# The tile stage of a gated attention and mixture-of-experts kernel: another order within a tile, no index copies, loops written out

## The chip, the cores and the metric

The kernel runs on one core of a Trainium2 chip. The metric is the device time of one execution in microseconds; for the kernel before it is the median of three runs, 376.43 us (375.81 to 379.23).

## What is computed

A block of a gated Flamingo layer over x, 8 x 256 x 256 floats: a retention attention on a normalised x, added to x through a tanh gate, then a mixture of 8 experts of which each token uses 2, added through a second gate. The change touches the second half only:

```python
scores = softmax(xf @ Wg.T); expert_weights, expert_indices = top_k(scores, 2)
gates = (one_hot(expert_indices, 8) * expert_weights[..., None]).sum(axis=1)
h1 = lora_in(xf, W1, b1, A1, B1)     # 256 -> 512, per expert
h3 = lora_in(xf, W3, b3, A3, B3)
g = silu(h1) * h3
y_e = lora_out(g, W2, b2, A2, B2)    # 512 -> 256
y = einsum('te,ted->td', gates, y_e)
x = x + tanh(g_ffn) * y
```

xf is the normalised x, 2048 tokens.

## The kernel before

The kernel has three stages. In the first, some 130 us, the attention runs batch by batch, and the experts' weights are loaded, their low-rank parts added, and each weight split into a high part (WH) and a low part (WL) that stay on the chip. Then a short routing step sorts the tokens by expert into 39 tiles of 128 token slots (NT_SLOTS), each tile for one expert; it leaves for tile i one column of row indices to gather (`gidx`), one of row indices to scatter to (`sidx`), and the expert's number (`eid`). The last slots may be padding.

The third is the tile stage, from 152 us on. For each tile:
- GpSimd gathers 128 normalised rows into `xg` (four buffers, XBUF; L735), three tiles ahead, and scatters a finished tile `ys` with an addition into the output rows (L747). A scatter waits for the landing of the one before it, since two tiles can add to one row. Ahead of each, the index column is copied to a small tile of its own (`gi` L732, `si` L743), and GpSimd waits for its copy.
- TensorE transposes x (`x_transposes`, L473), multiplies by the weights of h1 and of h3 (`up`, L483, each in three passes: xh and xl by WH, xb by WL), transposes g (`g_transposes`, L491) and multiplies by W2 (`down`, L500, gh, gl, gb).
- ScalarE makes xh and xb from the x transposes (L645, L646), gh from the g transposes and gb from gh (L651, L653), the silu (L662), and the bias of the result into `ys` (L669). The last waits for the scatter that still reads that one of the two ys buffers.
- VectorE makes xl (L997) and gl (L1001), adds the biases to h1 and h3 (L1006), multiplies them (L1012), works out the token's gate (L989, L991), and finishes `ys` (L1018).

Every engine runs its own list in the order written; semaphores join them. `tile_steps` writes 4 tiles, then a loop of 8 turns with 4 tiles each, then 3 tiles; in the loop the tile number is a register, and so are the values waited for. The order within tile i, as each engine has it (each works on parts of three tiles):
- TensorE: x transposes of i+1, up h1 of i, g transposes of i-1, up h3 of i, down of i-1.
- ScalarE: xh and xb of i+1, gh and gb of i-1, silu of i, bias of ys of i.
- VectorE: xl of i+1, gate of i+1, bias of h1 of i, gl of i-1, bias of h3 and product of i, ys of i-1.
- GpSimd: gather of i+3, scatter of i-1.

Of the kernel before, what the change touches and what calls it, by code (L numbers as in the profile page):

```python
# [29 lines left out]
U32 = mybir.dt.uint32  # L30
# [37 lines left out]
def flamingo(nc, x, ctxT, wqkv, tables, mask, gates_in, w_all, lora, biases, wgT, ident_in, consts, out):  # L68
# [9 lines left out]
    with whole:  # L78
# [78 lines left out]
        tiles = ExitStack()  # L157
        gi = [sb(tiles, f"gi{p}", [P, 1], U32) for p in range(2)]
        si = [sb(tiles, f"si{p}", [P, 1], U32) for p in range(2)]
        xg = [sb(tiles, f"xg{q}", [P, D + K]) for q in range(XBUF)]  # L160
# [39 lines left out]
        s_gates, s_gates_d, s_g0, s_gs = sem("s_gates"), sem("s_gates_d"), sem("s_g0"), sem("s_gs")  # L200
        s_gi, s_si = sem("s_gi"), sem("s_si")
        s_xg = [sem(f"s_xg{q}") for q in range(XBUF)]
# [22 lines left out]
        def tile_steps(engine, step):  # L225

            turns = (NT_SLOTS - XBUF - (XBUF - 1)) // XBUF
            for i in range(XBUF):
                step(i, i, i == 0, True)
            with engine.Fori(1, turns + 1) as r:  # L230
                for q in range(XBUF):
                    step(XBUF * r + q, q, False, True)
            for i in range(XBUF * (turns + 1), NT_SLOTS):
                step(i, i % XBUF, False, i + 1 < NT_SLOTS)

# [100 lines left out]
        def _(pe):  # L336
# [129 lines left out]
            def x_transposes(i, q):  # L466
                pe.wait_ge(s_xg[q], 16 * ((i - q) // XBUF + 1))
                if not isinstance(i, int) or i > 0:
# [42 lines left out]
            def read_expert(i, q):  # L511
                pe.reg_load(regs[q], eid[0:1, bass.ds(i, 1)])

            def tile(i, q, first, more):
                p = q % 2
                if more and not first:
                    x_transposes(i + 1, (q + 1) % XBUF)
                e = expert(q)
                up(pH1, i, p, e, 0, s_h1)
                if first:  # L520
                    x_transposes(1, 1)
                if not first:
                    g_transposes(i - 1)
                up(pH3, i, p, e, 1, s_h3)
# [14 lines left out]
        def _(act):  # L539
# [107 lines left out]

            def g_parts(i):
                act.wait_ge(s_gT, i + 1)
                pos_wait(act, s_y, i)  # L650
                nc.scalar.activation(gh[:], pG[:, :], ACT.Copy).then_inc(s_gh, 1)  # L651
                act.wait_ge(s_gh, i + 1)
                nc.scalar.activation(gb[:], gh[:].bitcast(F32), ACT.Copy).then_inc(s_gb, 1)  # L653

            def tile(i, q, first, more):
                p = q % 2
                if more:
                    x_parts(i + 1, 1 - p)
                if not first:
                    g_parts(i - 1)  # L660
                act.wait_ge(s_h1b, i + 1)
                nc.scalar.activation(h1[:], h1[:], ACT.Silu).then_inc(s_silu, 1)  # L662

                e = act.value_load(eid[0:1, bass.ds(i, 1)], min_val=0, max_val=E - 1)
                act.wait_ge(s_gs, i + 1)
                if not isinstance(i, int) or i >= 2:
                    settle(act)
                    act.wait_ge(s_scat[p], 16 * half(i, p))
# [6 lines left out]
            tile_steps(act, tile)  # L675
            g_parts(NT_SLOTS - 1)


        @block.gpsimd
        def _(pool):  # L680
# [44 lines left out]

            def gather(i, q):
                pos_wait(pool, s_xT, i - XBUF + 1)
                pos_wait(pool, s_gs, i - XBUF + 1)
                p = q % 2
                if not isinstance(i, int) or i >= 2:  # L730
                    pool.wait_ge(s_xg[(q + 2) % XBUF], 16 * ((i - 2 - (q + 2) % XBUF) // XBUF + 1))
                nc.gpsimd.tensor_copy(gi[p][:], gidx[:, bass.ds(i, 1)]).then_inc(s_gi, 1)  # L732
                pool.wait_ge(s_gi, i + 1)
                settle(pool)
                nc.gpsimd.indirect_dma_start(out=xg[q][:], out_offset=None, in_=xn2_d,  # L735
                                             in_offset=bass.IndirectOffsetOnAxis(ap=gi[p][:, 0:1], axis=0)
                                             ).then_inc(s_xg[q], 16)

            def scatter(i, p):

                if not isinstance(i, int) or i >= 1:
                    pool.wait_ge(s_scat[1 - p], 16 * ((i + p) // 2))
# [4 lines left out]
                nc.gpsimd.indirect_dma_start(out=out_rows, out_offset=bass.IndirectOffsetOnAxis(ap=si[p][:, 0:1], axis=0),  # L747
                                             in_=ys[p][:], in_offset=None, bounds_check=TOK - 1,
                                             oob_is_err=False, compute_op=ALU.add).then_inc(s_scat[p], 16)
# [3 lines left out]
            for i in range(XBUF - 1):  # L753
                gather(i, i)

            def tile(i, q, first, more):

                if not isinstance(i, int) or i + XBUF - 1 < NT_SLOTS:
                    gather(i + (XBUF - 1), (q + XBUF - 1) % XBUF)
                if not first:  # L760
                    scatter(i - 1, (q + 1) % 2)

            tile_steps(pool, tile)
            scatter(NT_SLOTS - 1, (NT_SLOTS - 1) % 2)


        @block.vector
        def _(dve):
# [216 lines left out]
            def gates_of(i, q):  # L985

                dve.wait_ge(s_xg[q], 16 * ((i - q) // XBUF + 1))
                pos_wait(dve, s_gs, i)
                nc.vector.tensor_tensor(g0, xg[q][:, D:D + 1], is0[:, bass.ds(i, 1)], ALU.mult).then_inc(s_g0, 1)  # L989
                dve.wait_ge(s_g0, i + 1)  # L990
                nc.vector.scalar_tensor_tensor(gs[q], xg[q][:, D + 1:D + 2], is1[:, bass.ds(i, 1)], g0,  # L991
                                               ALU.mult, ALU.add).then_inc(s_gs, 1)
# [119 lines left out]
```

## Time and profile before

| | us |
|---|---|
| median of three runs | 376.43 |
| the profiled execution | 375.73 |
| its span, first to last instruction | 373.9 |
| TensorE matmuls busy | 310.2 (83%) |
| VectorE busy | 262.3 (70%) |
| GpSimd busy | 209.6 (56%) |
| ScalarE busy | 186.1 (50%) |
| DMA in the chain that ended last | 34% |

The profile is of one execution. Engines are named PE (matmuls), PEld (TensorE's weight loads), DVE (VectorE), ACT (ScalarE), POOL (GpSimd). The granted TensorE clock is at its full level in the whole tile stage from 163 us on. A scatter or gather shows up twice: as an instruction on POOL, which is the time in which GpSimd writes out what is to be moved, and in the chain of waits as "DMA", from the start of that instruction to the landing of the data.

### The profile page before, as it was taken

To read this page: it belongs to the slowest core of one execution; us is meant where nothing else is said; L and a number is where in the kernel's file an instruction comes from. 1 tells how busy PE (TensorE), PEld (TensorE's weight loads), DVE (VectorE), ACT (ScalarE), POOL (GpSimd) and SP (SyncE) were. 2 spreads that over 40 slices of the span, in tenths; PEclk is the share of its full clock that TensorE was granted. 3 is DMA by queue.
4 is the path that set the end of the run, shared out by engine and by line. 5 is a ranking of instruction groups with operands and counts; after the bars stand their busy time and mean duration, and the time that the engine had idled before them with its cause. 6 is when DMAs were issued, how large, how long until landed. Compare 5 with 4: busy or idle time off the path is not lost.

```text
span 373.9 us, 7655 instructions
## 1 busy us (share of the span) xinstructions
PE 310.2 (83%) x1680; PEld 232.8 (62%) x1701; DVE 262.3 (70%) x639; ACT 186.1 (50%) x372; POOL 209.6 (56%) x247
## 2 busy tenths in 40 slices
PE   2869779989987723299999999999999999999970
PEld 1747667767766512157765777777777767677750
DVE  1667878898896689357675677776778767777750
ACT  4634645554655422065455555565555555455630
POOL 0456577777687436425465556656556556556441
PEclk9989999999998855579999999999999999999997
DMA  7779999678566449511332323322331323333200
GB/s 257 223 226 319 314 292 283 197 216 254 184 202 199 134 107 297 211 45 28 59 44 39 56 44 47 51 47 52 53 56 29 56 45 53 56 43 50 28 2 1
DMA packets 27887, 45.78 MB, mean 122 GB/s; under 512 B 6528, under 2 KB 15104, under 8 KB 27360
## 3 DMA queue, kind: packets, MB, share of 16 engines
q1 hardware_dynamic: 15408, 28.52, 24.2%
q0 software_dynamic: 7488, 9.36, 15.5%
q10 hardware_dynamic: 4976, 7.74, 6.9%
q8 instruction: 6, 0.10, 0.1%
q14 instruction: 9, 0.07, 0.1%
HBM read 33.65 MB, written 12.86 MB: 124 GB/s over the span
## 4 chain that ended last, share of the span: by engine, by line
DMA 34%; PE 20%; issue 13%; DVE 13%; ACT 7%; POOL 7%; POOLq 2%; DVEq 1%; SPq 1%; ACTq 0%
DMA out<-ys,si 26%; PE bank L483 3%; PE bank L393 3%; DMA LS<-lora_parts 3%; POOL WL L683 3%; PE bank L427 2%; PE bank L500 2%; DVE gl L1001 2%; DMA WH<-lora_in 2%; DVE h L1006 2%; PE bank L349 2%; DMA stage<-w_all_in 2%; DVE g L1006 1%; ACT xn L575 1%; PE bank L420 1%
## 5 line engine op out<-in xcount | busy, mean ns | idle before, releaser
L747 POOL DMA_INDIRECT out<-ys,si x39 | 62.5, 1603 | 45.8 <-POOL si L743 26.2
L683 POOL TENSOR_TENSOR WL<-stage,WH 128x512 f32 (+1 forms) x48 | 60.3, 1271 | 31.4 <-ACT WH L570 31.4
L735 POOL DMA_INDIRECT xg<-xn_rows,gi x39 | 39.5, 1013 | 32.6 <-POOL gi L732 32.6
L483 PE MATMUL bank<-WH,xh 128*128 x156 | 56.7, 445 | 0.7 <-ACT xh L645 0.7
L997 DVE TENSOR_TENSOR xl<-bank,xh 128x256 fp32r<-128x256 f32 x39 | 16.6, 425 | 48.6 <-ACT xb L646 48.6
L483 PE MATMUL bank<-WH,xl 128*128 x156 | 49.5, 399 | 0.0
L669 ACT ACTIVATE ys<-BB,gsel 128x256 f32 x39 | 19.8, 509 | 57.4 <-DMA out<-ys,si 57.1
L483 PE MATMUL bank<-WL,xb 128*128 x136 | 43.2, 388 | 1.6 <-issue 0.2
L570 ACT ACTIVATE WH<-stage 128x512 f32 (+1 forms) x48 | 29.0, 625 | 28.7 <-DVE stage L773 28.7
L651 ACT ACTIVATE gh<-bank 128x512 fp32r<-128x512 f32 x39 | 23.3, 598 | 26.5 <-PE bank L491 26.5
L483 PEld LDWEIGHTS bank<-WH,xl 128*128 128x128 f32 x156 | 29.8, 191 | 6.7 <-DVE xl L997 0.2
L773 DVE TENSOR_TENSOR stage<-bank,stage 128x512 f32<-128x512 f32 x48 | 31.3, 680 | 3.8 <-DMA stage<-w_all_in 2.9
L500 PE MATMUL bank<-WH,gh 128*128 x156 | 32.1, 328 | 0.9 <-ACT gh L651 0.9
L500 PE MATMUL bank<-WH,gl 128*128 x156 | 27.1, 296 | 3.7 <-DVE gl L1001 2.6
L1012 DVE TENSOR_TENSOR g<-g,h 128x512 f32<-128x512 f32 x39 | 27.0, 693 | 4.1
L732 POOL COPY gi<-gidx 128x1 uint32 (+1 forms) x39 | 27.2, 699 | 2.8 <-DVE sidx L980 2.7
L1006 DVE TENSOR_TENSOR h<-bank,BB 128x512 f32<-128x512 f32 x39 | 27.0, 691 | 2.5 <-PE bank L483 1.0
L500 PEld LDWEIGHTS bank<-WH,gh 128*128 128x128 f32 x156 | 24.0, 189 | 7.0 <-issue 1.8
L1006 DVE TENSOR_TENSOR g<-bank,BB 128x512 f32<-128x512 f32 x39 | 26.7, 686 | 1.9 <-PE bank L483 1.1
L1001 DVE TENSOR_TENSOR gl<-bank,gh 128x512 fp32r<-128x512 f32 x39 | 26.7, 683 | 2.0 <-ACT gh L651 1.5
L483 PEld LDWEIGHTS bank<-WH,xh 128*128 128x128 f32 x156 | 24.4, 193 | 2.7 <-issue 2.3
L500 PEld LDWEIGHTS bank<-WH,gl 128*128 128x128 f32 x156 | 20.9, 188 | 8.0 <-DVE gl L1001 7.7
(132 smaller groups left out, 619.3 us busy)
## 6 DMA issues: line engine op xcount, KB each, us to landing
stage<-w_all_in SPq DMA_DIRECT2D x48, 256.0 KB, 4.0
BB<-biases_in SPq DMA_DIRECT2D x8, 640.0 KB, 9.7
LS<-lora_parts SPq DMA_DIRECT2D x24, 144.0 KB, 3.0
lora_parts<-WH ACTq DMA_DIRECT2D x3, 864.0 KB, 9.4
xs<-x_in SPq DMA_DIRECT2D x8, 256.0 KB, 3.8
cx<-ctxT_in SPq DMA_DIRECT2D x8, 256.0 KB, 4.1
out<-x ACTq DMA_DIRECT2D x8, 256.0 KB, 2.3
xn_rows<-xn ACTq DMA_DIRECT2D x8, 256.0 KB, 4.2
```

Of the source, the lines that this page charges most:

```text
L483: last = nc.tensor.matmul(dst[:, :], lhs[p][:, c * P:(c + 1) * P], W[:, bass.ds(e * (UNITS * UC) + (2 * kind + c) * UC, HID)], start=(part ...
L500: last = nc.tensor.matmul(pY[:, 0:D], lhs[:, c * P:(c + 1) * P], W[:, bass.ds(e * (UNITS * UC) + 4 * UC + c * D, D)], start=(part == 0 and ...
L570: nc.scalar.activation(w_dst(WH, s, m), stage[(u * UNITS + m) % NSTAGE][:], ACT.Copy).then_inc(s_wh, 1)
L651: nc.scalar.activation(gh[:], pG[:, :], ACT.Copy).then_inc(s_gh, 1)
L683: nc.gpsimd.tensor_tensor(w_dst(WL, s, m), stage[(u * UNITS + m) % NSTAGE][:], w_dst(WH, s, m).bitcast(F32), ALU.subtract).then_inc(s_wl, 1)
L732: nc.gpsimd.tensor_copy(gi[p][:], gidx[:, bass.ds(i, 1)]).then_inc(s_gi, 1)
L735: nc.gpsimd.indirect_dma_start(out=xg[q][:], out_offset=None, in_=xn2_d, in_offset=bass.IndirectOffsetOnAxis(ap=gi[p][:, 0:1], axis=0)).th ...
L747: nc.gpsimd.indirect_dma_start(out=out_rows, out_offset=bass.IndirectOffsetOnAxis(ap=si[p][:, 0:1], axis=0), in_=ys[p][:], in_offset=None, ...
L773: nc.vector.tensor_tensor(stage[b][:], pW[m % 2][:, :], stage[b][:], ALU.add).then_inc(s_add, 1)
L1001: nc.vector.tensor_tensor(gl[:], pG[:, :], gh[:].bitcast(F32), ALU.subtract).then_inc(s_gl, 1)
L1006: nc.vector.tensor_tensor(dst[:], src[:, :], b, ALU.add).then_inc(sig, 1)
L1012: nc.vector.tensor_tensor(g[:], g[:], h1[:], ALU.mult).then_inc(s_g, 1)
```

## The change

1. `tile_steps` writes out all 39 tiles; tile numbers and the values waited for become constants. GpSimd's own loop likewise.
2. The index copies `gi` and `si` and their semaphores go; gather and scatter take a column of `gidx` and `sidx` directly. One of the gather's waits goes too.
3. The order within a tile:
   - TensorE: up h1 of i, g transposes of i-1, x transposes of i+1, up h3 of i, down of i-1.
   - ScalarE: gh of i-1, xh and xb of i+1, gb of i-1, then as before.
   - VectorE: gate of i+1, bias of h1, gl of i-1, xl of i+1, bias of h3 and product, ys of i-1.

```diff
         def tile_steps(engine, step):
 
-            turns = (NT_SLOTS - XBUF - (XBUF - 1)) // XBUF
-            for i in range(XBUF):
-                step(i, i, i == 0, True)
-            with engine.Fori(1, turns + 1) as r:
-                for q in range(XBUF):
-                    step(XBUF * r + q, q, False, True)
-            for i in range(XBUF * (turns + 1), NT_SLOTS):
-                step(i, i % XBUF, False, i + 1 < NT_SLOTS)
+            for i in range(NT_SLOTS):
+                step(i, i % XBUF, i == 0, i + 1 < NT_SLOTS)
...
             def tile(i, q, first, more):
                 p = q % 2
-                if more and not first:
-                    x_transposes(i + 1, (q + 1) % XBUF)
-                e = expert(q)
-                up(pH1, i, p, e, 0, s_h1)
-                if first:
-                    x_transposes(1, 1)
+                up(pH1, i, p, expert(q), 0, s_h1)
                 if not first:
                     g_transposes(i - 1)
-                up(pH3, i, p, e, 1, s_h3)
+                if more:
+                    x_transposes(i + 1, (q + 1) % XBUF)
+                up(pH3, i, p, expert(q), 1, s_h3)
...
-            def g_parts(i):
+            def g_high(i):
                 act.wait_ge(s_gT, i + 1)
                 pos_wait(act, s_y, i)
                 nc.scalar.activation(gh[:], pG[:, :], ACT.Copy).then_inc(s_gh, 1)
+
+            def g_short(i):
                 act.wait_ge(s_gh, i + 1)
                 nc.scalar.activation(gb[:], gh[:].bitcast(F32), ACT.Copy).then_inc(s_gb, 1)
 
             def tile(i, q, first, more):
                 p = q % 2
+                if not first:
+                    g_high(i - 1)
                 if more:
                     x_parts(i + 1, 1 - p)
                 if not first:
-                    g_parts(i - 1)
+                    g_short(i - 1)
...
-            def gather(i, q):
-                pos_wait(pool, s_xT, i - XBUF + 1)
-                pos_wait(pool, s_gs, i - XBUF + 1)
-                p = q % 2
-                if not isinstance(i, int) or i >= 2:
-                    pool.wait_ge(s_xg[(q + 2) % XBUF], 16 * ((i - 2 - (q + 2) % XBUF) // XBUF + 1))
-                nc.gpsimd.tensor_copy(gi[p][:], gidx[:, bass.ds(i, 1)]).then_inc(s_gi, 1)
-                pool.wait_ge(s_gi, i + 1)
-                settle(pool)
+            def gather(i):
+
+                q = i % XBUF
+                if i >= XBUF:
+                    pool.wait_ge(s_xT, i - XBUF + 1)
+                    pool.wait_ge(s_gs, i - XBUF + 1)
                 nc.gpsimd.indirect_dma_start(out=xg[q][:], out_offset=None, in_=xn2_d,
-                                             in_offset=bass.IndirectOffsetOnAxis(ap=gi[p][:, 0:1], axis=0)
+                                             in_offset=bass.IndirectOffsetOnAxis(ap=gidx[:, i:i + 1], axis=0)
                                              ).then_inc(s_xg[q], 16)
 
-            def scatter(i, p):
-
-                if not isinstance(i, int) or i >= 1:
+            def scatter(i):
+
+                p = i % 2
+                if i >= 1:
                     pool.wait_ge(s_scat[1 - p], 16 * ((i + p) // 2))
-                nc.gpsimd.tensor_copy(si[p][:], sidx[:, bass.ds(i, 1)]).then_inc(s_si, 1)
-                pool.wait_ge(s_si, i + 1)
                 pool.wait_ge(s_ys, i + 1)
-                settle(pool)
...
             def tile(i, q, first, more):
                 p = q % 2
-                e = dve.value_load(eid[0:1, bass.ds(i, 1)], min_val=0, max_val=E - 1)
+                e = dve.value_load(eid[0:1, i:i + 1], min_val=0, max_val=E - 1)
                 if more:
-                    x_rest(i + 1, 1 - p)
                     gates_of(i + 1, (q + 1) % XBUF)
                 pos_wait(dve, s_g, i)
                 biased(h1, pH1, i, e, 0, s_h1, s_h1b)
                 if not first:
                     g_rest(i - 1)
+                if more:
+                    x_rest(i + 1, 1 - p)
                 product(i, e)
```

## Rows read from the trace of the kernel before

**Rows 1.** The page: busy time by engine, and the chain by line.
```profile
PE 310.2 (83%) x1680; PEld 232.8 (62%) x1701; DVE 262.3 (70%) x639; ACT 186.1 (50%) x372; POOL 209.6 (56%) x247
...
DMA out<-ys,si 26%; PE bank L483 3%; PE bank L393 3%; DMA LS<-lora_parts 3%; POOL WL L683 3%; PE bank L427 2%; PE bank L500 2%; DVE gl L1001 2%; DMA WH<-lora_in 2%; DVE h L1006 2%; PE bank L349 2%; DMA stage<-w_all_in 2%; DVE g L1006 1%; ACT xn L575 1%; PE bank L420 1%
```

**Rows 2.** Chain of waits around 220 us: start us, us, what.
```profile
217.67 0.46 DVE ys L1018
...
219.01 3.78 DMA out<-ys,si
...
222.94 0.19 POOL si L743
...
224.06 3.81 DMA out<-ys,si
```

**Rows 3.** Timeline of TensorE, 270 to 280 us: start us, us, instructions merged.
```profile
270.12 0.60 PE L491 MATMUL bank<-ident,g 128*128 128x128 f32 x4
...
272.40 0.64 PE L500 MATMUL bank<-WH,gl 128*128 x4
272.88 0.61 PE L500 MATMUL bank<-WL,gb 128*128 x4
...
273.47 0.72 PE L483 MATMUL bank<-WH,xh 128*128 x2
...
274.94 0.60 PE L491 MATMUL bank<-ident,g 128*128 128x128 f32 x4
```

**Rows 4.** Timeline of TensorE, 279 to 285 us.
```profile
280.19 0.60 PE L491 MATMUL bank<-ident,g 128*128 128x128 f32 x4
...
283.35 0.61 PE L500 MATMUL bank<-WL,gb 128*128 x4
...
284.35 0.73 PE L483 MATMUL bank<-WH,xh 128*128 x2
```

**Rows 5.** Timeline of TensorE, first and last but one g transposes.
```profile
165.47 0.66 PE L491 MATMUL bank<-ident,g 128*128 128x128 f32 x4
...
356.51 0.60 PE L491 MATMUL bank<-ident,g 128*128 128x128 f32 x4
```

**Rows 6.** Waits of weight loads, 165 to 357 us: total us, times, longest.
```profile
PEld bank L500 <- DVE gl L1001: 7.7, 20, 1.0
```

**Rows 7.** Timeline of ScalarE and VectorE, 270 to 277 us; in brackets idle time before.
```profile
271.56 0.68 DVE L1001 TENSOR_TENSOR gl<-bank,gh 128x512 fp32r<-128x512 f32 x1
...
274.15 0.51 ACT L669 ACTIVATE ys<-BB,gsel 128x256 f32 x1 [1.61 <-DMA out<-ys,si]
...
275.57 0.60 ACT L651 ACTIVATE gh<-bank 128x512 fp32r<-128x512 f32 x1 [0.37 <-PE bank L491]
...
276.76 0.68 DVE L1001 TENSOR_TENSOR gl<-bank,gh 128x512 fp32r<-128x512 f32 x1
```

**Rows 8.** Timeline of GpSimd: a scatter, the gather behind it, the last scatter.
```profile
275.29 1.61 POOL L747 DMA_INDIRECT out<-ys,si  x1 [0.93 <-POOL si L743]
...
277.93 1.01 POOL L735 DMA_INDIRECT xg<-xn_rows,gi  x1 [0.84 <-POOL gi L732]
...
365.61 1.57 POOL L747 DMA_INDIRECT out<-ys,si  x1 [1.23 <-issue]
```

**Rows 9.** Timeline of GpSimd: the first gather.
```profile
153.60 1.17 POOL L735 DMA_INDIRECT xg<-xn_rows,gi  x1 [1.00 <-POOL gi L732]
```

**Rows 10.** Chain of waits, 180 to 204 us: the two late landings.
```profile
180.70 4.72 DMA out<-ys,si
...
196.90 5.67 DMA out<-ys,si
```

**Rows 11.** DMA queues, 152 to 374 us: the queue of code: packets, MB, share.
```profile
q8 instruction: 4, 0.07, 0.1%
```

**Rows 12.** DMA queues, 183 to 184 us.
```profile
q8 instruction: 1, 0.02, 7.6%
```

**Rows 13.** Chain of waits, 360 to 374 us: the last scatter but one.
```profile
361.38 2.76 DMA out<-ys,si
```

More of the change, by code:

```diff
@@ L157, in flamingo @@
         tiles = ExitStack()
-        gi = [sb(tiles, f"gi{p}", [P, 1], U32) for p in range(2)]
-        si = [sb(tiles, f"si{p}", [P, 1], U32) for p in range(2)]
         xg = [sb(tiles, f"xg{q}", [P, D + K]) for q in range(XBUF)]
@@ L200, in flamingo @@
         s_gates, s_gates_d, s_g0, s_gs = sem("s_gates"), sem("s_gates_d"), sem("s_g0"), sem("s_gs")
-        s_gi, s_si = sem("s_gi"), sem("s_si")
         s_xg = [sem(f"s_xg{q}") for q in range(XBUF)]
@@ L467, in x_transposes @@
                 pe.wait_ge(s_xg[q], 16 * ((i - q) // XBUF + 1))
-                if not isinstance(i, int) or i > 0:
+                if i > 0:
                     pe.wait_ge(s_xh, i)
@@ L511, in read_expert @@
             def read_expert(i, q):
-                pe.reg_load(regs[q], eid[0:1, bass.ds(i, 1)])
+                pe.reg_load(regs[q], eid[0:1, i:i + 1])
             def tile(i, q, first, more):
                 p = q % 2
-                if more and not first:
-                    x_transposes(i + 1, (q + 1) % XBUF)
-                e = expert(q)
-                up(pH1, i, p, e, 0, s_h1)
-                if first:
-                    x_transposes(1, 1)
+                up(pH1, i, p, expert(q), 0, s_h1)
                 if not first:
                     g_transposes(i - 1)
-                up(pH3, i, p, e, 1, s_h3)
+                if more:
+                    x_transposes(i + 1, (q + 1) % XBUF)
+                up(pH3, i, p, expert(q), 1, s_h3)
                 if more:
@@ L659, in tile @@
                 if not first:
-                    g_parts(i - 1)
+                    g_short(i - 1)
                 act.wait_ge(s_h1b, i + 1)
                 nc.scalar.activation(h1[:], h1[:], ACT.Silu).then_inc(s_silu, 1)
-                e = act.value_load(eid[0:1, bass.ds(i, 1)], min_val=0, max_val=E - 1)
+                e = act.value_load(eid[0:1, i:i + 1], min_val=0, max_val=E - 1)
                 act.wait_ge(s_gs, i + 1)
-                if not isinstance(i, int) or i >= 2:
-                    settle(act)
+                if i >= 2:
                     act.wait_ge(s_scat[p], 16 * half(i, p))
@@ L675, in _ @@
             tile_steps(act, tile)
-            g_parts(NT_SLOTS - 1)
+            g_high(NT_SLOTS - 1)
+            g_short(NT_SLOTS - 1)
         @block.gpsimd
@@ L723, in _ @@
                                         ALU.mult).then_inc(s_atj, 1)
-            def gather(i, q):
-                pos_wait(pool, s_xT, i - XBUF + 1)
-                pos_wait(pool, s_gs, i - XBUF + 1)
-                p = q % 2
-                if not isinstance(i, int) or i >= 2:
-                    pool.wait_ge(s_xg[(q + 2) % XBUF], 16 * ((i - 2 - (q + 2) % XBUF) // XBUF + 1))
-                nc.gpsimd.tensor_copy(gi[p][:], gidx[:, bass.ds(i, 1)]).then_inc(s_gi, 1)
-                pool.wait_ge(s_gi, i + 1)
-                settle(pool)
+            def gather(i):
[3 more added lines that the diff above has]
+                    pool.wait_ge(s_gs, i - XBUF + 1)
                 nc.gpsimd.indirect_dma_start(out=xg[q][:], out_offset=None, in_=xn2_d,
-                                             in_offset=bass.IndirectOffsetOnAxis(ap=gi[p][:, 0:1], axis=0)
+                                             in_offset=bass.IndirectOffsetOnAxis(ap=gidx[:, i:i + 1], axis=0)
                                              ).then_inc(s_xg[q], 16)
-            def scatter(i, p):
-                if not isinstance(i, int) or i >= 1:
+            def scatter(i):
+                p = i % 2
+                if i >= 1:
                     pool.wait_ge(s_scat[1 - p], 16 * ((i + p) // 2))
-                nc.gpsimd.tensor_copy(si[p][:], sidx[:, bass.ds(i, 1)]).then_inc(s_si, 1)
-                pool.wait_ge(s_si, i + 1)
                 pool.wait_ge(s_ys, i + 1)
-                settle(pool)
-                nc.gpsimd.indirect_dma_start(out=out_rows, out_offset=bass.IndirectOffsetOnAxis(ap=si[p][:, 0:1], axis=0),
+                nc.gpsimd.indirect_dma_start(out=out_rows, out_offset=bass.IndirectOffsetOnAxis(ap=sidx[:, i:i + 1], axis=0),
                                              in_=ys[p][:], in_offset=None, bounds_check=TOK - 1,
@@ L753, in _ @@
             for i in range(XBUF - 1):
[L754 to L764, printed above, removed]
+                gather(i)
+            for i in range(NT_SLOTS):
+                if i + XBUF - 1 < NT_SLOTS:
+                    gather(i + XBUF - 1)
+                if i >= 1:
+                    scatter(i - 1)
+            scatter(NT_SLOTS - 1)
         @block.vector
@@ L988, in gates_of @@
                 pos_wait(dve, s_gs, i)
-                nc.vector.tensor_tensor(g0, xg[q][:, D:D + 1], is0[:, bass.ds(i, 1)], ALU.mult).then_inc(s_g0, 1)
+                nc.vector.tensor_tensor(g0, xg[q][:, D:D + 1], is0[:, i:i + 1], ALU.mult).then_inc(s_g0, 1)
                 dve.wait_ge(s_g0, i + 1)
-                nc.vector.scalar_tensor_tensor(gs[q], xg[q][:, D + 1:D + 2], is1[:, bass.ds(i, 1)], g0,
+                nc.vector.scalar_tensor_tensor(gs[q], xg[q][:, D + 1:D + 2], is1[:, i:i + 1], g0,
                                                ALU.mult, ALU.add).then_inc(s_gs, 1)
```

## Prediction, made before the changed kernel was run

> **What bounds the kernel now.** I read the page first: TensorE is busy for 83% of the span, yet the largest item of the chain that ended last is the landing of the scatter, 26% [rows 1]. Both can't be the bound alone, so I went to the tile stage, the stretch that the change touches, and read the chain of waits there, then each engine's timeline.
>
> The chain shows a loop that closes on itself [rows 2]. A scatter starts at 219.01 and lands 3.78 us later, at 222.79; GpSimd then copies the index (0.19), and the next scatter starts at 224.06, 5.05 us after the first. So landing to start is 1.27 us with the index copy. Where the scatter is released by VectorE's ys instead, ys ends at 218.13 and the scatter starts at 219.01: 0.88 us with no copy between. The loop is serial by its own wait (scatter i waits for scatter i-1).
>
> TensorE has a loop of its own. The reader should compare the starts of the g transposes, one set per tile [rows 3, 4]: 270.12 to 274.94 is 4.82 us, 274.94 to 280.19 is 5.25. The long tile is one in which gl came late; in the stage 20 of TensorE's weight loads waited for gl, 7.7 us in all [rows 6]. At the back edge of the written loop there is another loss: the last matmuls of down start at 283.35 and the next up at 284.35, 1.00 us, where the same step takes 0.59 inside a turn (272.88 to 273.47): 0.41 us in each of 8 turns. The mean distance over the stage, from 165.47 to 356.51 for 37 distances, is 191.04 / 37 = 5.16 us [rows 5]; the best are 4.8.
>
> Why gl is late [rows 7]: ScalarE is in order, and its ys for the tile (274.15) waits for a scatter's landing; behind it stand xh and xb, behind these VectorE's xl, the two gate operations, the bias of h, and only then gl (276.76 to 277.44). Relative to the g transposes gl ends 2.50 us later here, and 2.12 in the unstalled tile (272.24 - 270.12), where TensorE starts on it after 2.28. So the serial scatters (5.05 us) bound the stage, and TensorE (4.8) follows close behind.
>
> **The change part by part.** The sum is made against the profiled execution, 375.73 us (span 373.9 and 1.8 around it); the median of the runs shown, 376.43, is 0.7 above it.
>
> Index copy out of the scatter. Landing to start falls from 1.27 to about 0.88 us, as where ys released it and no copy lay between [rows 2]; the register move and the dispatch stay. The loop becomes 3.80 + 0.88 = 4.68 us against 5.05. Bounds: at least the copy itself goes (0.19, loop 4.86); at most half of what is left of the 0.88 goes too (loop 4.3). I take 4.68, the nearest row.
>
> Index copy out of the gather. The gather takes 1.01 us and starts 2.64 us after the scatter (275.29, 277.93) [rows 8]. It lies under the scatter's 3.8 us landing and costs nothing in either version; without that cover it would cost about 1.8 us a tile. Without the copy it can start at the end of the scatter's own 1.61, which is what rival C is about. At the entry the first gather loses its copy (0.19, as the scatter's) and the 1.00 idle behind it [rows 9] shrinks towards the 0.88 above: -0.3 us, on the path to the first tile.
>
> Loops written out. The 0.41 at each back edge goes (8 x 0.41 = 3.3 us, part of the difference between 5.16 and 4.8, not added to it). Register arithmetic for i, branches and the extra semaphore increments go too. TensorE reads the expert's register twice per tile, one short move more, covered by matmuls (bounds 0 and 0.05 x 39 = 2 us; I take 0, since such moves stand between matmuls now without a gap). What is added is code to fetch; see below.
>
> The new order. Count from the g transposes of a tile. TensorE: g transposes 0, x transposes 0.35, up of h3 about 0.55, gh 1.85, gl 2.5, gb 3.0, next up 3.45, g transposes again 4.8: the same instructions as before, so the same 4.8. ScalarE: gh starts at 0.63 as now (275.57 - 274.94) and ends at 1.23; xh and xb follow to 1.8, gb (as long as gh) to 2.4, needed at 3.0; silu to 3.1. VectorE: the gates; the bias of h from 0.2 to 0.9, since it no longer stands behind xl; gl (0.68) from 1.26 to 1.95, needed at 2.5; then xl, needed only at 4.1 by the next up; bias of h3 when its matmuls end (2.05 to 2.7); product to 3.5, needed at 4.8; result when the last gb matmul has ended, to 4.1. VectorE is busy for 4 us of a tile, below 4.8. What stands behind the moved waits: behind ScalarE's wait for the g transposes the x parts, with 2 us to spare; behind VectorE's wait for xb the bias of h3 and the product, with 0.4 and 1.3.
>
> How late may a scatter be? With ys ended at 4.1 it starts at 5.0 and lands at 8.8; ScalarE's ys behind it ends at 9.5, its next gh is due at 9.6 + 0.63 = 10.2: 0.75 us to spare there and 0.55 at gl, 1.3 in all before TensorE stalls.
>
> Code to fetch. The stage has 11 tile bodies of code for its 39 tiles (4, a loop of 4, 3), and four fetches of 16 KB fall in it [rows 11]; with 39 bodies it is about 14. What one can do [rows 10, 12]: a fetch lies at 183 us in a scatter's data, and that scatter landed after 4.72 us instead of 3.8; the one of 196.90 landed after 5.67, with a fetch in its wait too. The other two fetches cost no landing. So I estimate that half of 14 hit, 7 x 0.9 = 6.3 us late in all. Cover: 1.3 us once and 34 x (4.79 - 4.68) = 3.7 us that the shorter scatter loop makes up. Left: 1.3; with one hit of the dearer kind (0.9 more) 2.2, so a tile costs 4.79 + 0.06 = 4.85.
>
> A page of the Trainium skill, "Runtime: NRT & Kernel Launch", section "Instruction fetch mechanics", says that code is streamed ahead in 16 KiB blocks and that crossing a block is mostly hidden, while a taken branch outside the window stalls. By that rule the stage would take 37 x 4.79 = 177.2 us and the kernel 361.7. The trace agrees for TensorE, which shows no gap at 183 us, and not for the scatter (4.72).
>
> The end. The last scatter but one starts at 361.38 and lands 2.76 later, at 364.14; the last starts at 365.61, 1.47 after that [rows 8, 13]. With 0.88 it starts 0.6 earlier. The 8.3 us behind it (to 373.9) are untouched.
>
> Sum: entry -0.3; stage 37 x 4.85 = 179.4 against 191.0, -11.6; end -0.6: **-12.5 us**. 375.73 - 12.5 = 363.2, and with the 0.7 between that execution and the median 363.9 us.
>
> **The rivals.**
> A, every large fetch hits a scatter: 14 x 0.9 = 12.6 us late, 5.0 covered, 7.6 left on 177.2. The stage takes 184.8, -6.2, and the kernel 376.4 - 6.2 - 0.9 = 369.3. For it: blocks may follow each other at the same phase of every third tile. Against it: two of four hit now.
> B, no change: each fetch costs a scatter 1.4 on average, between the two that are seen (0.9, 1.9): 19.6 - 5.0 = 14.6, the stage 191.8, and the kernel 376.3. The same comes out if any wait of the new order makes each tile 0.3 us late.
> The skill's page "DMA: Bandwidth & Descriptors", section "Queues, rings and completion order", says that an engine takes turns between its queues packet by packet; by it a scatter's small packet can stand behind 16 KB, and A and B stay open. The 4.72 agrees.
> C, slower: the gather starts right behind the scatter, 1.6 us after it instead of 2.64, and its rows mix with the scatter's. Price: up to 1.0 us a landing, the time by which it moves. At 0.75 the scatter loop is 3.8 + 0.75 + 0.88 = 5.43 against 5.16, 34 x 0.27 = +9.2, -0.9 at the ends: 384.7. It decides from 0.5 a landing, where the loop is 5.18. Against it: one engine issues both to one queue, the scatter first.
>
> **How the numbers follow.** My forecast 0.60 (own range 361 to 367), A 0.18, B 0.12, C 0.10. The predicted time is 363.9. The low end is that of no fetch cost, 361.7, and 0.06 us a tile less on TensorE (2.2 us), since up of h1 no longer begins on the x transposes: 359.5. The high end takes in A and a quarter of the way on to B: 371. About 1% (3.8 us) is what a measurement of this kernel can tell from no change: faster is my case and A, 0.78; the same is B, 0.12; slower is C, 0.10.
>
> **What would show it.** Right: distances between g transposes of 4.8 to 4.9, no weight load waiting for gl, landing to next scatter 0.9, landings still 3.8 but scatters often released by ys; some 14 fetches of 16 KB, the long tiles beside them. Wrong: landings above 4.3 in every tile (C); scatter distances of 5.1 with a late landing every third tile (A, B); TensorE gaps before loads that nothing in the trace released.

## The result, and the profile after

| | before | after |
|---|---|---|
| median, us | 376.12 (4 runs) | 363.69 (4 runs, 361.68 to 365.32) |
| ratio | | 0.965, 95% interval 0.958 to 0.972 |
| the profiled execution | 375.73 | 365.32 |
| its span | 373.9 | 363.5 |

The changed kernel is 12.4 us faster. The profiled execution of it happens to be the longest of the four, which matters below. The ratios below leave out slow executions (over 1.5% above the fastest of their kernel) and the medians do not, and the profiles of no_copies_old_order (372.49 us) and pe_loop (367.11) are of slow ones.

The page, busy time by engine and the chain by line:

```profile
PE 305.6 (84%) x1680; PEld 232.8 (64%) x1700; DVE 266.3 (73%) x638; ACT 179.2 (49%) x371; POOL 192.6 (53%) x169
...
PE bank L474 29%; PE bank L491 15%; PE bank L482 5%; PE bank L418 4%; PE bank L384 3%; PE bank L464 2%; POOL WL L675 2%; DMA WH<-lora_in 2%; PE bank L340 2%; PE bank L411 2%; PE bank L393 1%; PE bank L429 1%; DMA LS<-lora_parts 1%; DVE WH L798 1%; ACT xn L563 1%
```

Where the scatter's landing held 26% of the chain [rows 1], it is gone from the list, and up (L474), down (L491) and the g transposes (L482) stand in its place. The chain of waits around 275 us (start us, us, what) is TensorE alone, where [rows 2] had one scatter after another:

```profile
273.20 1.38 PE bank L474 x6
274.58 0.44 PE bank L482 x4
275.02 0.22 PE bank L464 x2
275.24 1.39 PE bank L474 x6
276.63 1.41 PE bank L491 x12
278.04 1.38 PE bank L474 x6
279.42 0.44 PE bank L482 x4
```

These pieces close without a gap: 274.58 to 279.42 is one tile, 4.84 us. VectorE and ScalarE of the same tile show the new order (timeline; in brackets the idle time before and what ended it):

```profile
274.17 0.51 ACT L660 ACTIVATE ys<-BB,gsel 128x256 f32 x1 [1.75 <-DMA out<-ys,sidx]
...
274.42 0.60 PE L482 MATMUL bank<-ident,g 128*128 128x128 f32 x4
...
274.81 0.69 DVE L989 TENSOR_TENSOR h<-bank,BB 128x512 f32<-128x512 f32 x1 [0.42 <-PE bank L474]
...
275.06 0.60 ACT L639 ACTIVATE gh<-bank 128x512 fp32r<-128x512 f32 x1 [0.38 <-PE bank L482]
...
275.69 0.69 DVE L984 TENSOR_TENSOR gl<-bank,gh 128x512 fp32r<-128x512 f32 x1 [0.19 <-ACT gh L639]
...
276.31 0.43 DVE L980 TENSOR_TENSOR xl<-bank,xh 128x256 fp32r<-128x256 f32 x1
...
276.95 0.64 PE L491 MATMUL bank<-WH,gl 128*128 x4
```

gl ends 1.96 us after the g transposes began (276.38 - 274.42) and TensorE starts on it after 2.53; before it ended after 2.50 in a stalled tile [rows 7]. ScalarE's ys still waits for a scatter (1.75 us), but the wait now ends 0.9 us ahead of gh. GpSimd's timeline:

```profile
195.72 1.59 POOL L734 DMA_INDIRECT out<-ys,sidx  x1 [1.95 <-DVE gsel L974]
197.61 0.99 POOL L724 DMA_INDIRECT xg<-xn_rows,gidx  x1 [0.31 <-issue]
201.88 1.59 POOL L734 DMA_INDIRECT out<-ys,sidx  x1 [3.28 <-DMA out<-ys,sidx]
203.78 0.99 POOL L724 DMA_INDIRECT xg<-xn_rows,gidx  x1 [0.30 <-issue]
206.51 1.59 POOL L734 DMA_INDIRECT out<-ys,sidx  x1 [1.75 <-DMA out<-ys,sidx]
```

The gather follows its scatter after 1.89 us instead of 2.64 [rows 8]. The scatter of 195.72 is a late one: its landing took 5.3 us, so the next one, at 201.88, is late too. The one after that, at 206.51, already makes up for it: 4.63 us behind the one before, where TensorE's tile takes 4.83.

Where the 10.4 us between the two spans went, by the same marks (first gather; first and last but one g transposes; last scatter):

| stretch | before | after | difference |
|---|---|---|---|
| start to first gather | 153.6 | 155.3 | +1.7 |
| to the first g transposes | 11.9 | 11.1 | -0.8 |
| 37 distances of g transposes | 191.0 | 180.5 | -10.6 |
| to the last scatter | 9.1 | 8.4 | -0.7 |
| to the end | 8.3 | 8.2 | 0 |

The first row mixes two things. The gather's copy is gone, which took 1.0 us off (see the entry below); the code before it is the same in both kernels and took 2.7 us more in this execution, which is not the change's. Over all profiled executions of this study the first gather started after 151.6 to 158.7 us. The -0.8 of the second row is not firm either: the same kernel once more took 12.0 us there (after_again, below). So I compare kernels by the 37 distances, and by medians only where several us are at stake.

### The profile page after: what moved, and what is told of

Its sections match the earlier page's. It is cut to its first block, busy times and chain, and to the rows that moved or that the text cites. A ratio compares the mean times of both kernels' runs of the same rounds, so it can differ in the third digit from the quotient of the medians.

```text
span 363.5 us, 7072 instructions
## 1 busy us (share of the span) xinstructions
PE 305.6 (84%) x1680; PEld 232.8 (64%) x1700; DVE 266.3 (73%) x638; ACT 179.2 (49%) x371; POOL 192.6 (53%) x169
## 4 chain that ended last, share of the span: by engine, by line
PE 69%; DVE 7%; POOL 5%; DMA 5%; issue 5%; ACT 4%; SPq 1%; ACTq 1%; POOLq 1%; DVEq 0%
PE bank L474 29%; PE bank L491 15%; PE bank L482 5%; PE bank L418 4%; PE bank L384 3%; PE bank L464 2%; POOL WL L675 2%; DMA WH<-lora_in 2%; PE bank L340 2%; PE bank L411 2%; PE bank L393 1%; PE bank L429 1%; DMA LS<-lora_parts 1%; DVE WH L798 1%; ACT xn L563 1%
## 5 line engine op out<-in xcount | busy, mean ns | idle before, releaser
L734 POOL DMA_INDIRECT out<-ys,sidx x39 | 61.8, 1585 | 88.4 <-DVE gsel L974 58.0
L474 PE MATMUL bank<-WH,xh 128*128 x156 | 56.5, 443 | 0.7 <-ACT xh L633 0.7
L474 PE MATMUL bank<-WH,xl 128*128 x156 | 49.2, 397 | 0.0
L724 POOL DMA_INDIRECT xg<-xn_rows,gidx x39 | 38.7, 992 | 15.5 <-issue 11.3
L474 PE MATMUL bank<-WL,xb 128*128 x136 | 43.0, 386 | 1.6 <-issue 0.2
L984 DVE TENSOR_TENSOR gl<-bank,gh 128x512 fp32r<-128x512 f32 x39 | 27.0, 691 | 10.6 <-ACT gh L639 10.6
L474 PEld LDWEIGHTS bank<-WH,xl 128*128 128x128 f32 x156 | 29.5, 189 | 7.4 <-DVE xl L980 0.2
L491 PE MATMUL bank<-WH,gh 128*128 x156 | 32.2, 328 | 1.0 <-ACT gh L639 0.9
L491 PEld LDWEIGHTS bank<-WH,gh 128*128 128x128 f32 x156 | 24.0, 189 | 7.8 <-issue 2.7
L474 PEld LDWEIGHTS bank<-WH,xh 128*128 128x128 f32 x156 | 23.9, 192 | 2.3 <-issue 1.8
L643 ACT ACTIVATE gb<-gh 128x512 bf16<-128x512 f32 x39 | 25.0, 641 | 0.1
L654 ACT ACTIVATE h<-h 128x512 f32<-128x512 f32 x39 | 25.0, 641 | 0.0
L482 PEld LDWEIGHTS bank<-ident,g 128*128 128x128 f32 x156 | 19.3, 140 | 8.8 <-DVE g L995 1.7
L491 PE MATMUL bank<-WH,gl 128*128 x156 | 24.9, 281 | 0.0
```

Source lines behind the costliest of these rows:

```text
L474: last = nc.tensor.matmul(dst[:, :], lhs[p][:, c * P:(c + 1) * P], W[:, bass.ds(e * (UNITS * UC) + (2 * kind + c) * UC, HID)], start=(part ...
L482: last = nc.tensor.transpose(pG[:, c * P:(c + 1) * P], g[:, c * P:(c + 1) * P], ident[:])
L491: last = nc.tensor.matmul(pY[:, 0:D], lhs[:, c * P:(c + 1) * P], W[:, bass.ds(e * (UNITS * UC) + 4 * UC + c * D, D)], start=(part == 0 and ...
L984: nc.vector.tensor_tensor(gl[:], pG[:, :], gh[:].bitcast(F32), ALU.subtract).then_inc(s_gl, 1)
```

## The experiments

Two questions: which part of the change carried the gain, and whether the account of two loops (scatters in series, TensorE close behind) is what happens. Each number of "37 distances" is from the first to the last but one g transposes in TensorE's timeline, as in [rows 5], in one profiled execution of each kernel. A late landing is one of more than 4.3 us.

### One part at a time

**order_only**: the kernel before with the new order in its loops; TensorE, ScalarE and VectorE as in the change, the rest untouched.

```diff
                 p = q % 2
-                if more and not first:
-                    x_transposes(i + 1, (q + 1) % XBUF)
-                e = expert(q)
-                up(pH1, i, p, e, 0, s_h1)
+                up(pH1, i, p, expert(q), 0, s_h1)
                 if not first:
                     g_transposes(i - 1)
+                if more:
+                    x_transposes(i + 1, (q + 1) % XBUF)
...
```

> Only the new order within a tile; loops and index copies stay as before. Theory (two loops, the longer sets the tile: scatters in series at 5.06 us with the copy, TensorE at 4.8): the scatter loop is untouched, so a tile still takes 5.06 to 5.1 instead of 5.16, gl is no longer late, and the gain is 2 to 4 us: 372 to 374 us. Rival (the order alone is what brought the gain, by freeing gl): 363 to 366 us, tiles of 4.85.

**written_out**: the kernel before with tile_steps written out; copies and order stay.

```diff
-            with engine.Fori(1, turns + 1) as r:
-                for q in range(XBUF):
-                    step(XBUF * r + q, q, False, True)
...
+            for i in range(NT_SLOTS):
+                step(i, i % XBUF, i == 0, i + 1 < NT_SLOTS)
```

> Only the loops written out; copies and old order stay. Theory: the back edge's 0.41 us on TensorE goes, but the scatters still follow each other every 5.06 us, and late landings beside code fetches are no longer made up: no gain, 374 to 378 us. Rival (loop control was the cost): 8 x 0.41 = 3.3 us and more off, 370 to 372 us with tiles below 5.0.

**written_order**: both of these; only the index copies, and with them the semaphore increment behind each copy (`settle`) and one of the gather's waits, differ from the changed kernel.

> Loops written out and the new order, but the index copies kept: the whole change but one part. Theory: the scatter loop with its copy (1.27 us from landing to start) sets the tile, 5.06 us, 371 to 375 us. Rival (the copies were hidden): as the changed kernel, 362 to 365 us, tiles of 4.83.

**no_copies_old_order**: the changed kernel with the old order on the three engines.

```diff
                 if more:
+                    x_rest(i + 1, 1 - p)
                     gates_of(i + 1, (q + 1) % XBUF)
                 pos_wait(dve, s_g, i)
                 biased(h1, pH1, i, e, 0, s_h1, s_h1b)
                 if not first:
                     g_rest(i - 1)
-                if more:
-                    x_rest(i + 1, 1 - p)
...
```

> Loops written out and copies gone, but the old order within a tile. Theory: scatters can follow each other every 4.65 us, TensorE sets the tile at 4.8 to 4.9 if gl comes in time, since ScalarE's ys is released earlier: 363 to 367 us, some loads still waiting for gl. Rival (the order is needed for TensorE to run without stalls): tiles above 5.0, 369 us or more.

| kernel | written out | copies gone | new order | 37 distances | a tile, mean | median us | ratio (interval) |
|---|---|---|---|---|---|---|---|
| before | | | | 191.0 | 5.16 | 375.67 | |
| order_only | | | x | 190.9 | 5.16 | 378.57 | 1.003 (0.998 to 1.009) |
| written_out | x | | | 186.8 | 5.05 | 373.85 | 0.989 (0.978 to 1.000) |
| written_order | x | | x | 186.8 | 5.05 | 372.86 | 0.992 (0.988 to 0.996) |
| no_copies_old_order | x | x | | 183.8 | 4.97 | 367.14 | 0.972 (0.963 to 0.982) |
| after | x | x | x | 180.5 | 4.88 | 363.69 | 0.965 (0.958 to 0.972) |

The order alone gains nothing, twice (190.9 against 191.0, 186.8 against 186.8): TensorE's freedom is of no use while scatters come every 5 us. The rival that put the gain on the order falls, but so does my own figure for order_only, 5.06 to 5.1 a tile and 2 to 4 us less; it had 5.16 and no gain. Its GpSimd shows why:

```profile
276.97 1.61 POOL L749 DMA_INDIRECT out<-ys,si  x1 [0.94 <-POOL si L745]
278.00 1.32 POOL L734 COPY gi<-gidx 128x1 uint32 x1
280.15 1.01 POOL L737 DMA_INDIRECT xg<-xn_rows,gi  x1 [0.83 <-POOL gi L734]
281.17 0.20 POOL L745 COPY si<-sidx 128x1 uint32 x1
282.31 1.60 POOL L749 DMA_INDIRECT out<-ys,si  x1 [0.94 <-POOL si L745]
```

The gather's index copy takes up to 1.33 us here; it took 0.77 in the kernel before. So the gather ends up to 4.2 us after the scatter's start (281.16 - 276.97), behind the landing at 3.8 and not ahead of it, and holds up the next scatter, which came 5.34 us after the one before. The prediction had the gather cost nothing because it lies under the landing; in order_only it does not fit under it. Why the copy is longer stays open. That 190.9 equals 191.0 is then partly chance: the kernel before had landings of 4.7 and 5.7 us in its profile, order_only none above 4.3.

Taking out the copies is worth 6.3 us with the new order and 3.0 with the old; and once they are gone the order is worth 3.3. These are single executions, and late landings are in them: the changed kernel once more had 178.8 us (after_again, below), which makes it 8.0 for the copies and 5.0 for the order, and the medians do not part the last two rows of the table clearly. For no_copies_old_order I had expected 4.8 to 4.9 a tile, and the rival tiles above 5.0; 4.97 lies between. In its waits what is left is the old pattern, smaller:

```profile
DVE xl L978 <- ACT xb L637: 39.0, 37, 2.1
...
PEld bank L491 <- DVE gl L982: 2.6, 7, 0.9
PE bank L491 <- DVE gl L982: 1.3, 3, 0.7
```

(total us, times, longest; 170 to 350 us.) No weight load waits for gl any more in the changed kernel.

My expectation for written_out was wrong: I had no gain in the stage, and it has 4.3 us. The time from landing to the next scatter shows why: it falls from 1.27 to 1.17 us although the copy and the semaphore increment behind it stay. From the end of the copy to the scatter it is 0.94 us in both; the 0.1 lies ahead of the copy, where the loop works out in a register what to wait for. I had counted that as free. 37 x 0.1 = 3.7 us is most of the 4.3. In the median the gain is not clear of noise (interval up to 1.000).

### Are there two loops?

**no_gb**: the changed kernel without the third pass of down, so less exact: 4 matmuls fewer per tile on TensorE, nothing else shorter.

```diff
-                for part, (lhs, W, ready) in enumerate(((gh, WH, s_gh), (gl, WH, s_gl), (gb, WL, s_gb))):
+                for part, (lhs, W, ready) in enumerate(((gh, WH, s_gh), (gl, WH, s_gl))):
...
-                                                start=(part == 0 and c == 0), stop=(part == 2 and c == HC - 1))
+                                                start=(part == 0 and c == 0), stop=(part == 1 and c == HC - 1))
```

> The changed kernel without the third pass of down (gb by WL, 4 matmuls of 256 columns a tile), so its output is less exact; ScalarE still makes gb. Theory (two loops, TensorE 4.83 and scatters 4.65 close behind): TensorE needs 4.38 us a tile, but the scatters now set it: distances of 4.65 to 4.7, 37 of them in 172 to 174 us. Rival (TensorE is the only bound): 4.38 us, 162 to 163 us for the 37.

37 distances took 170.5 us, 4.61 a tile; the shortest tiles took 4.36. Median 353.57 us. That is 1.5 us below the range I gave and far above the rival's 162 to 163. The chain of waits has gone back to the scatters:

```profile
238.88 3.69 DMA out<-ys,sidx
...
242.62 0.56 issue
...
243.39 3.85 DMA out<-ys,sidx
...
247.29 0.56 issue
...
248.06 3.39 DMA out<-ys,sidx
```

243.39 - (238.88 + 3.69) = 0.82 us from landing to scatter, and 4.5 to 4.7 a tile: the scatter loop without copies, 0.2 below TensorE's 4.83.

**no_gb_reg**: the same with the scatter's row bound in a register that is set once. With a constant, each scatter is preceded by a register move, and GpSimd's waits stand ahead of the move.

```diff
+            last_row = pool.alloc_register("last_row")
+            pool.reg_mov(last_row, TOK - 1)
...
-                                             in_=ys[p][:], in_offset=None, bounds_check=TOK - 1,
+                                             in_=ys[p][:], in_offset=None, bounds_check=last_row,
```

> As no_gb (third pass of down left out, output less exact), and the scatter's bound is kept in a register set once, so that no register move stands between GpSimd's waits and the scatter. Theory (of the 0.82 us from landing to the next scatter 0.55 lie behind that move, and the first gather of the changed kernel, which waits with no move behind the wait, started 0.27 us after its release): landing to start falls to 0.3 us, the scatter loop to 4.1 to 4.2, TensorE's 4.37 sets the tile: 37 distances in 161.5 to 163.5 us instead of 170.5. Rival (the dispatch takes 0.8 whatever stands before it): 4.6 us as in no_gb.

163.6 us, 4.42 a tile on average and 4.37 in most of them; median 346.98 us, 6.6 less than no_gb. From landing to scatter it is now 0.27 us where the landing is what releases it. Where the scatter waits for its ys instead, it still starts 0.82 us after ys has ended (0.89 with the register move): the wait for ys is an instruction of its own ahead of the DMA. So one instruction between the landing and the DMA, on an engine that is busy half the time, was worth 0.2 us a tile, and with it gone TensorE sets the tile again. Both halves of the account are shown: shorten TensorE and the scatters bound, shorten the scatters and TensorE bounds.

**reg_bounds**: the same register in the changed kernel, with all passes.

> The changed kernel with the scatter's bound in a register set once. Theory: landing to start 0.3 us instead of 0.82; TensorE's 4.83 sets the tile with or without it, so the stage stays at 178.7 to 180 us, and only the last scatters gain, 0.5 us: 361 to 364 us. Rival (the scatter loop still costs the changed kernel time in most tiles): 3 us or more less.

179.1 us, 4.84 a tile; median 362.61. No gain in the stage, as the account wants: the path that it shortens has slack. The 0.5 us I expected at the end did not come either: last but one g transposes to last scatter took 8.29 us against 8.36. The last scatter then waits for its ys, and on that side the register is worth only 0.07 us. One tile took 5.12 us, behind a landing of 5.1.

### What code fetches do

The changed kernel's stage has the fetches that were estimated (queue of code, 152 to 364 us; packets, MB):

```profile
q8 instruction: 13, 0.21, 0.4%
```

against 4 [rows 11]. In its profile three scatters landed after 5.3 us, those of 195.72, 225.26 and 254.84. A 16 KB fetch was on its way 3 us after each of them had started, and behind each stands a tile of 5.4 us; every other tile between 166 and 347 us is 4.82 to 4.88.

**after_again**: the changed kernel once more.

> The changed kernel itself once more, as the neighbour of the next three. Theory: tiles of 4.83 us with two or three of 5.4, each behind a scatter that landed after some 5.3 us; 37 distances in 179 to 181 us; 361 to 366 us in all. Rival (the long tiles of the first profile were chance): none above 5.0.

178.8 us for the 37; median 362.42 us, ratio 0.961 (0.953 to 0.969). It had one late landing, of 4.7 us, and no tile above 4.9. That is neither of my cases: the long tiles come with the late landings, but how many there are differs from one execution to the next, with the same 13 fetches. When a fetch falls matters most. In the first 35 scatters of all thirteen traces, as far as their landings are recorded, 21 had a 16 KB fetch start 1.75 to 2.7 us after their own start, and every one landed late or nearly so, after 4.28 to 5.32 us. Of 33 with a fetch at 2.7 to 3.8 us nine took 5.2 to 6.0. Of 27 with a fetch earlier none took above 4.0; of 343 with no fetch before their landing two took above 4.3 (4.32 and 4.37).

**ys3**: a third ys buffer, so that ScalarE waits for the scatter of three tiles before.

```diff
+        yv = [ys[0][:], ys[1][:], cst[:, 0:D]]
...
-                if i >= 2:
-                    act.wait_ge(s_scat[p], 16 * half(i, p))
-                nc.scalar.activation(ys[p][:], BB[...], ACT.Copy,
+                if i >= 3:
+                    act.wait_ge(s_scat[(i - 3) % 2], 16 * ((i - 3) // 2 + 1))
+                nc.scalar.activation(yv[i % 3], BB[...], ACT.Copy,
```

> The changed kernel with three buffers for ys instead of two (the third lies over the routing constants, dead by then), so that ScalarE waits for the scatter of three tiles before instead of two. Theory (a late landing reaches TensorE through ScalarE's wait before ys, xh, gh): landings of 5.3 us still occur but no tile is above 5.0, the 37 distances take 178.7 to 179.2 us, 1 to 2 us less than with two buffers. Rival (the code fetch itself holds up TensorE): tiles of 5.4 stay.

This execution had seven late landings, up to 6.0 us (the row: DMA to landing, min, median, max), and no tile above 4.9: 178.8 us for the 37. Median 361.90 us.

```profile
DMA to landing us min/median/max: 2.7/3.8/6.0
...
264.80 0.60 PE L483 MATMUL bank<-ident,g 128*128 128x128 f32 x4
269.64 0.60 PE L483 MATMUL bank<-ident,g 128*128 128x128 f32 x4
274.46 0.60 PE L483 MATMUL bank<-ident,g 128*128 128x128 f32 x4
...
265.97 1.59 POOL L735 DMA_INDIRECT out<-cst,sidx  x1 [1.30 <-DMA out<-ys,sidx]
...
272.77 1.59 POOL L735 DMA_INDIRECT out<-ys,sidx  x1 [3.92 <-DMA out<-cst,sidx]
```

The scatter of 265.97 is the worst of the study, the next could start only 6.80 us later, and the g transposes beside it keep 4.84 and 4.82. So the fetch does not hold up TensorE; a late landing does, by way of ScalarE's wait for the ys buffer, and one buffer more cuts that way. It does not make the lateness go away: 33 of the scatters waited for the landing before them, they stayed behind to the end, and from the last but one g transposes to the last scatter it took 9.3 us instead of 8.4. The medians of ys3 and the changed kernel (361.90, 362.42) can't be told apart. In the changed kernel with two buffers the same way is seen at work: ScalarE's ys at 201.24 had waited 3.0 us, and its gh came 0.8 us late (1.40 us behind the g transposes of 200.25, where 0.64 is usual), with gl after it.

```profile
201.24 0.51 ACT L660 ACTIVATE ys<-BB,gsel 128x256 f32 x1 [2.99 <-DMA out<-ys,sidx]
201.65 0.58 ACT L639 ACTIVATE gh<-bank 128x512 fp32r<-128x512 f32 x1
```

**pe_loop**: the changed kernel, TensorE alone in its loop of 8 turns.

```diff
-            tile_steps(pe, tile)
+            looped_steps(pe, tile)
...
+        def looped_steps(engine, step):
+
+            turns = (NT_SLOTS - XBUF - (XBUF - 1)) // XBUF
+            for i in range(XBUF):
+                step(i, i, i == 0, True)
+            with engine.Fori(1, turns + 1) as r:
+                for q in range(XBUF):
+                    step(XBUF * r + q, q, False, True)
...
```

> The changed kernel, but TensorE alone keeps its loop of 8 turns with 4 tiles. Theory (late landings come from TensorE's 16 KB code fetches; the back edge costs TensorE 0.3 to 0.4 us): 4 such fetches in the stage instead of 13, at most one landing above 5 us, but 8 tiles of 5.1 to 5.25; the 37 distances take 181.5 to 183 us, 1 to 2.5 us more than written out. Rival (landings are late for another reason): as many late landings as before. Second rival (the back edge is covered): no tile of 5.1 and 179 us.

4 fetches of 16 KB, no scatter of a full tile above 4.3 us, 179.9 us for the 37; median 363.04 us, ratio 0.960 (0.952 to 0.969). One tile in four is 4.96 to 5.04 instead of 4.83:

```profile
211.41 0.60 PE L493 MATMUL bank<-ident,g 128*128 128x128 f32 x4
216.25 0.60 PE L493 MATMUL bank<-ident,g 128*128 128x128 f32 x4
221.25 0.60 PE L493 MATMUL bank<-ident,g 128*128 128x128 f32 x4
226.08 0.60 PE L493 MATMUL bank<-ident,g 128*128 128x128 f32 x4
```

So the back edge costs 0.17 us a turn (221.25 - 216.25 against 4.83), 1.2 us in all, not the 0.3 to 0.4 of my expectation, and the 37 are below its 181.5. TensorE's loop takes 9 of the 13 fetches away, so these 16 KB fetches are TensorE's code. The one late landing, 4.5 us for a padding tile's scatter at 347.86 (2.7 is usual), has one of the four remaining fetches in it, at 350.1. With the count over all traces above I take it as shown that late landings come with these fetches; what in the transfers holds the scatter up no run shows. In the time of the whole kernel written-out TensorE code and a loop come out the same here.

### The best version

**ys3_reg**: third ys buffer and register bound together.

> Three ys buffers and the bound in a register: the candidate for the best version. Theory: no long tile whatever lands late, 178.7 us for the 37 distances in every execution, the end 0.5 us shorter than the changed kernel's: 360 to 363 us. Rival: no different from the changed kernel within 0.3%.

178.8 us for the 37, two late landings (5.2 and 5.0) and no long tile; median 360.41 us, ratio 0.959 (0.944 to 0.974). It is the lowest median of the kernels that compute the whole result, but its interval covers that of the changed kernel, so all that can be said is that it is not worse. The end did not get shorter than the changed kernel's (8.28 us from the last but one g transposes to the last scatter), but it is 1.0 below that of ys3, whose scatters had fallen behind.

## Why the prediction was right, point by point

**The forecast**, 363.9 us, against 363.69; the range held. The mechanism, two loops of which the scatters were the longer by 0.25 us and TensorE the next, is shown by order_only (no gain on the wrong loop), no_gb and no_gb_reg. That the number fits to 0.2 us is luck: the same kernel once more had a median of 362.42, and the terms were off in both directions (entry -1.0 for -0.3, stage -10.6 in the first profile and -12.2 in the second for -11.6).

**Landing to next scatter**: forecast 0.88 us, measured 0.82; the row it was taken from is one of a release by ys, and there the changed kernel has 0.89. The scatter loop is 4.5 to 4.7 (forecast 4.68).

**The gather** was put at nothing because it lies under the landing. That holds in the changed kernel, where it ends 2.88 us after the scatter's start (195.72, 197.61 + 0.99), and not in order_only, where it ended after up to 4.2.

**TensorE's tile** was taken as 4.79, the best tiles of before; it is 4.82 to 4.84 in the new order. Why it is 0.04 longer (1.5 us in all) stays open. The second read of the expert's register, which I had put at nothing with 2 us as its bound, does not explain it: no_copies_old_order reads it once and has no full tile below 4.82, order_only and written_order read it twice and have tiles of 4.81.

**Code fetches**: 0.06 us a tile was allowed; the first profile has 4.88 - 4.83 = 0.05, the second none. The sum was right but its parts were not. I had half of 14 fetches make a landing 0.9 late. Seen were three at 1.5, one at 0.9, or seven of up to 2.2. And the cover "1.3 us before TensorE stalls" was too large: a landing 1.5 late (5.3) made a tile 0.58 longer (5.41), so 0.95 is covered. If the 0.75 that I gave ScalarE holds, only 0.2 of gl's 0.55 is there; I take it that a late gh stops TensorE itself, which goes through gh before gl.

**The entry** was the worst-sized term in proportion. I gave the first gather -0.3 us, from 1.24 to 0.9 after the routing's last operation, with the scatter's 0.88 as the nearest row. The chain of waits of the changed kernel:

```profile
154.88 0.18 DVE sidx L963
155.06 0.27 issue
155.33 3.01 DMA xg<-xn_rows,gidx
```

It is 0.27, so -1.0: the gather has no register move behind its wait, and no_gb_reg has the same 0.27 for a scatter without one. The scatter's row was not the nearest after all: the two differ by exactly the piece that costs most.

**The back edge** was put at 0.41 us a turn from the trace of before. pe_loop shows 0.17 where TensorE alone has the loop. That the x transposes, then at the start of the turn, made up the rest is not shown: in order_only they are in mid-tile, every engine has its loop, and the step from down to up still takes 0.86 us at a back edge (283.24 to 284.10) against 0.53 in the tile before. It was not added to the sum, so it did no harm.

**The split** between the parts was left open by the prediction, which gave one figure for the stage. The runs give 4.3 us to the loops (mostly through the scatter's path, not through TensorE's as the text had it), 3.0 to 8.0 to the copies, and 0 to 5.0 to the order, by what else is there and which execution is taken.

**The end**: -0.6 forecast, -0.7 measured.

**The rivals.** A and B (fetches eat 5 us or all of it) needed most fetches to hit; in the changed kernel's profiles three and one of 13 did. C (the gather in among the scatter's rows) did not occur: the gather starts 1.89 us after the scatter, 0.75 earlier than before, and landings stay at a median of 3.8 us.

**The page on instruction fetch** ("Runtime: NRT & Kernel Launch" of the Trainium skill, section "Instruction fetch mechanics": crossing a block is mostly hidden) is borne out for the engine that fetches: 13 blocks of 16 KB and TensorE's tiles stay at 4.83 in ys3. The kernel's own transfers are not left alone by those blocks: scatters beside them landed after up to 6.0 us instead of 3.8. The stage of 177.2 us that I worked out by that rule came out as 178.8 in after_again and ys3.

## What to carry to other kernels

When two loops are nearly as long, price a change by the one that sets the period, and ask how far behind the next one is: here the tile could fall from 5.16 us to TensorE's own 4.83 and no further (0.33 us), and freeing the second loop first gained nothing. In a chain "wait, then DMA" on GpSimd, look at what stands between the wait and the DMA: an index copy (with its own wait) or a register move there is paid in full in each turn in which that wait ends last, on an engine that is idle for half the time. Where an engine waits for a buffer that a serial transfer still reads, one buffer more than the average needs keeps a late landing away from it, since the late landing stalls and not the mean. Look at the end of the stage then, where the transfers that fell behind are paid for (1 us in ys3).

## What the runs showed of the hardware

- The scatter starts 0.27 us after the landing that releases it in no_gb_reg, and 0.82 in no_gb, where a register move stands between; the first gather of the changed kernel, with none, starts 0.27 after its release. Released by ys, a scatter starts 0.82 after its end in no_gb_reg and 0.89 in the changed kernel.
- An index column can be read where it lies: with a constant column number the gather and the scatter took slices of a 39-column tile, and their own times did not change (1.59 against 1.60 us, 0.99 against 1.01).
- A scatter with addition of 128 rows of 1 KB lands in 3.8 us, and in 2.7 when its tile is padding and no row is moved (the last ones of the stage).
- The number of late landings of one and the same kernel varied: three of up to 5.4 us in one execution, one of 4.7 in another. Every scatter with a 16 KB fetch starting 1.75 to 2.7 us after it landed after 4.28 us or more (21 of 21).
- The first 150 us, the same code in all kernels, took up to 7 us more or less from one profiled execution to another (first gather at 151.6 to 158.7 us). The granted clock goes with a part of it at most: the two executions with no half-speed stretch in their first 115 us came to it at 152.3 and 151.6 (no_gb_reg, ys3_reg), the four with 10.2 us at half speed there at 153.0 to 158.7, but written_out and pe_loop, with 3.4, at 156.6 and 156.5. The cause is open.
